# Cross attention's context keys and values: made per chunk in the cross stage, or for all chunks during the first chunks of attention and kept in memory

## The chip, the cores and the metric

One core of a Trainium2 chip. The metric is the device time of one execution in microseconds (us). Engines are named as in the profile: PE is TensorE's matrix multiplications and PEld its weight loads, DVE is VectorE, ACT ScalarE, POOL GpSimd, SP SyncE, which here issues most DMAs. Each engine runs its own instructions strictly in the order of its program and waits only on semaphores.

## What is computed

128 sequences of 64 tokens with 128 features (8192 tokens), all in f32, go through four residual steps. Cut to what matters:

```python
x = x + tanh(g_xattn[0]) * L0_xattn(layernorm(x), ctx)   # per token: 16 heads attend over each other
x = x + tanh(g_ffn[0])   * L0_ffn(layernorm(x))          # 2 of 8 experts, chosen by a sum of features
x = x + tanh(g_xattn[1]) * L1_xattn(layernorm(x), ctx)   # cross attention, 64 x 64 within a sequence
x = x + tanh(g_ffn[1])   * L1_ffn(layernorm(x))          # 2 shared units and 8 gated ones

# L1_xattn(vis, lang):
vis_key   = vis  @ W_vk.T + b_vk
lang_key  = lang @ W_lk.T + b_lk          # depends on the context alone
vis_value = vis  @ W_vv.T + b_vv
lang_value = lang @ W_lv.T + b_lv         # depends on the context alone
attn = softmax(vis_key @ lang_key.T * scale)
return attn @ lang_value + attn @ (attn.T @ vis_value)
```

The kernel computes the last line as attn @ (lang_value + attn.T @ vis_value).

## The kernel before

The tokens are cut into 16 chunks of 512 (`NC` = 16, `CH` = 512), four sequential 128-token tiles each. Four steps are staged over a common count of **half ticks** (`for half in range(2 * TICKS)`, with `tick = half // 2` and `later = half % 2`), and every engine runs its own copy of this loop. The order of the work on each engine is written out by these loops; engines meet only at semaphores, so a half tick is a place in the order and not a time.

- **Attention** (`a_part`, L95): chunk a takes half ticks 16(a+1) to 16(a+1)+15, and k is the place in it (0 to 15). The next chunk (p) and the one before (r) have places in the same sixteen. On PE (`attention`, `tail_uses` L119) k = 3 makes `ot` of chunk r (it waits for DVE's `head_scale`, L906, at k = 2) and the first half of keys and values of p, k = 5 makes `wo` of r (the output projection, L1341 and L1240) and the second half, k = 7 `xt0`, k = 10 `q`, k = 13 `rank`. DVE takes `wo` at k = 6 (`attended`, L913) to form the residual, and goes on with `norm_stats`; POOL needs these statistics at k = 8 (L562) before its products of the second half (L586).
- **Experts** of block b (four chunks): from half tick 108 (block 0) up to half tick 356, after a planned table (`PLACE`). Lines L1276 and L1290 on PE, L683 on ACT, L1014 on DVE. Their weights are loaded by SP.
- **Cross attention** of chunk c: from tick `C0[c]` = 136, 144, ..., 256, so 8 ticks for each chunk. PE's steps (`cross`, `C_FIRST` and `C_LATER`): `lk` (L1391, tick 0), `xt2` (tick 0, later half), `vk` (L1397, tick 1), `sc` (L1404, tick 1), `vv` (L1240, tick 2), `bdt`, `val` (L1415 and L1416 by turns, tick 4), `att` (L1422, tick 5), `xt3` (tick 7). ACT copies `lk` out of PSUM with its bias (L672). DVE adds the row bias to `val` (`biased`, L1019, into `u_sb`).
- **Units** of chunk c (the last step, 10 of them): from tick `C0[c]` + 8. PE L1244 to L1246 and L1326/L1328, ACT L705, DVE L1095 and L1110. DVE's `ut_lo` (L1188) comes ahead of unit 0.

The attention steps outside the experts and most cross steps share two PSUM banks, `M[0]` (MA) and `M[1]` (MC). `bank_uses` gives the cross steps these banks by turns, and each `fill` waits until the use before it in the same bank is drained. `ZB[0]` and `ZB[1]` are used for splitting the unit weights up to half tick 30 and then lie unused until the experts begin.

For cross attention SP loads chunk c of the context into `ctx2_t` (L515) two ticks ahead of `C0[c]`. The profile joins buffers whose names differ by numbers: `ctx_t` in its rows is also `ctx2_t`, `xn` also `xn2`.

## Time and profile before

| | us |
|---|---|
| runs (three) | 1303.09, 1305.31, 1306.69; median 1305.31 |
| the profiled execution's own time | 1305.32 |
| its span in the trace | 1303.6 |
| PE busy | 1113.0 (85%) |
| DVE busy | 1010.9 (78%) |
| ACT busy, POOL busy | 586.5 (45%), 637.0 (49%) |

Times in rows are counted from the span's start. A row of a timeline has: start us, us, engine, line, operation, out<-in, forms, count, and in brackets the idle time before it on its engine with what ended it. One f32 matrix multiplication is recorded as two. The rows of busy time by stretch give PE, PEld, DVE, ACT and POOL in this order, each with its instructions, then the clock. "PEclk" is the granted TensorE clock as a share of 2.4 GHz. For reading by time, four stretches: attention alone (to about 236 us), attention with experts (to about 630), experts with cross attention and units (to about 948), cross attention and units (to the end).

### The profile page before, as it was taken

The page shows a single profiled execution, that of the slowest core. Times are in us where ns is not written, and L with a number is a line of the kernel's source. Part 1 is how long each engine was busy: PE and PEld are TensorE (multiplying, and loading weights), DVE is VectorE, ACT ScalarE, POOL GpSimd, SP SyncE. Part 2 cuts the span into 40 slices and gives each one's busy share as a digit, 9 for nine tenths or more (in the row PEclk, how much of TensorE's full clock was granted, in tenths as well). Part 3 has the DMA queues.
Part 4 walks back from the last instruction along what each step waited for, and adds up shares of the span by engine and source line. Part 5 has one row for each costly group of instructions (what it writes and reads, how often), then busy time and mean ns, then how long its engine had stood idle before and what let it go on. Part 6 is the DMA issues. An engine that isn't in the chain of part 4 may idle for free.

```text
span 1303.6 us, 23736 instructions
## 1 busy us (share of the span) xinstructions
PE 1113.0 (85%) x7464; PEld 960.2 (74%) x7464; DVE 1010.9 (78%) x2393; ACT 586.5 (45%) x1506; POOL 637.0 (49%) x377
## 2 busy tenths in 40 slices
PE   5145544899969998799889999999999999999998
PEld 3133333789858988688788888889888888888887
DVE  2999999989999899898537444445688888888887
ACT  2212222465636555355454645454344444444443
POOL 4889997898788987899340110101011111111200
PEclk9999985799989999799899999999999999999999
DMA  6101112889748886589666255552000000000000
GB/s 226 49 25 41 40 41 73 264 269 284 224 151 263 278 253 208 187 240 294 189 198 206 78 176 160 174 162 79 22 25 25 25 25 25 26 25 25 26 9 17
DMA packets 125035, 166.41 MB, mean 128 GB/s; under 512 B 10032, under 2 KB 67568, under 8 KB 124912
## 3 DMA queue, kind: packets, MB, share of 16 engines
q1 hardware_dynamic: 119792, 152.31, 38.1%
q0 software_dynamic: 5120, 12.59, 2.9%
q8 instruction: 61, 1.00, 0.3%
q14 instruction: 62, 0.51, 0.1%
HBM read 137.60 MB, written 27.26 MB: 126 GB/s over the span
## 4 chain that ended last, share of the span: by engine, by line
PE 56%; DVE 25%; issue 8%; POOL 7%; ACT 2%; DMA 1%; SPq 0%; DVEq 0%; POOLq 0%; ACTq 0%
PE ZB L1276 8%; DVE q_sb L898 6%; PE YB L1290 6%; PE YD L1328 5%; DVE s L873 4%; PE ZD L1244 4%; PE ZD L1246 4%; PE ZD L1245 4%; POOL prod L586 3%; PE YB L1328 3%; PE ZB L1244 2%; DVE own_prod L862 2%; PE ZB L1246 2%; PE ZB L1245 2%; POOL xs L596 2%
## 5 line engine op out<-in xcount | busy, mean ns | idle before, releaser
L562 POOL TENSOR_TENSOR rstd<-ve,neghalf 128x4 f32<-128x4 f32 x64 | 65.6, 1025 | 516.6 <-DVE ve L827 515.2
L683 ACT ACTIVATE hid<-ZB,w2b 128x128 f32<-128x128 f32 x768 | 215.8, 378 | 159.0 <-PE YB L1290 78.5
L574 POOL TENSOR_TENSOR prod<-q_sb,kv_sb 128x2048 f32<-128x2048 f32 x48 | 216.3, 4507 | 51.9 <-DVE q_sb L898 31.6
L586 POOL TENSOR_TENSOR prod<-s,kv_sb 128x2048 f32<-128x2048 f32 x48 | 215.2, 4505 | 10.6 <-DVE q_sb L898 10.5
L1276 PE MATMUL ZB<-bt,w1b 128*128 128x128 f32 x1536 | 213.2, 284 | 4.9 <-ACT hid L683 4.7
L1276 PEld LDWEIGHTS ZB<-bt,w1b 128*128 128x128 f32 x1536 | 197.0, 200 | 8.5 <-issue 8.0
L1290 PE MATMUL YB<-w2b,hid 128*128 128x128 f32 x1024 | 141.4, 282 | 0.0
L1290 PEld LDWEIGHTS YB<-w2b,hid 128*128 128x128 f32 x1024 | 129.1, 194 | 14.2 <-ACT hid L683 8.0
L705 ACT ACTIVATE own_prod<-ZD 128x512 f32<-128x512 f32 x102 | 61.1, 599 | 154.6 <-PE ZD L1246 152.3
L1095 DVE TENSOR_TENSOR prod<-own_prod,ZD 128x512 f32<-128x512 f32 x102 | 69.5, 682 | 75.0 <-ACT own_prod L705 51.7
L1110 DVE SCALAR_TENSOR_TENSOR own_prod<-YD,gate,own_prod 128x128 f32<-128x128 f32 x320 | 89.7, 342 | 46.5 <-PE YD L1328 44.6
L873 DVE TENSOR_REDUCE s<-prod 128x256 f32<-128x2048 f32 x48 | 108.2, 2275 | 5.4 <-POOL prod L574 5.4
L898 DVE TENSOR_REDUCE q_sb<-prod 128x128 f32<-128x2048 f32 x48 | 109.1, 2273 | 1.4 <-POOL prod L586 1.0
L1244 PE MATMUL ZD<-ut_hi,w_hi 128*128 128x512 f32 x204 | 89.0, 436 | 0.0
L1328 PEld LDWEIGHTS YD<-w2u_sb,prod 128*128 128x128 f32 x640 | 79.8, 192 | 9.9 <-issue 4.7
L1328 PE MATMUL YD<-w2u_sb,prod 128*128 128x128 f32 x640 | 85.0, 276 | 2.4 <-DVE own_prod L1110 1.5
L1246 PE MATMUL ZD<-ut_lo,w_hi 128*128 128x512 f32 x204 | 80.5, 394 | 0.0
L1245 PE MATMUL ZD<-ut_hi,w_lo 128*128 128x512 f32 x204 | 80.4, 394 | 0.0
L596 POOL DMA_INDIRECT xs<-xrow,slots x64 | 63.3, 989 | 23.1 <-issue 17.7
L608 POOL DMA_INDIRECT x<-x2d,homes x64 | 61.8, 966 | 23.6 <-issue 23.3
L1290 PE MATMUL ZD<-w2b,hid 128*128 128x128 f32 x512 | 69.3, 279 | 0.0
L1290 PEld LDWEIGHTS ZD<-w2b,hid 128*128 128x128 f32 x512 | 62.6, 192 | 5.8 <-issue 3.0
(249 smaller groups left out, 2321.0 us busy)
## 6 DMA issues: line engine op xcount, KB each, us to landing
w2b<-in_w SPq DMA_DIRECT2D x96, 516.0 KB
w1b<-in_w SPq DMA_DIRECT2D x96, 512.0 KB
xb<-xs SPq DMA_DIRECT2D x96, 128.0 KB
ctx_t<-in_ctx SPq DMA_DIRECT2D x32, 256.0 KB
x2d<-x2s SPq DMA_DIRECT2D x48, 128.0 KB
x<-in_x SPq DMA_DIRECT2D x16, 256.0 KB
xs<-zrow SPq DMA_DIRECT2D x4, 1024.0 KB, 10.5
xrow<-in_x SPq DMA_DIRECT2D x16, 256.0 KB, 3.6
```

Of the source, the lines that this page charges most:

```text
L574: pool.tensor_tensor(out=prod[:, t % 2, :].rearrange("p (h e d) -> p h e d", h=HEADS, e=HEADS), in0=q.unsqueeze(2).broadcast_to([P, HEADS, ...
L586: pool.tensor_tensor(out=prod[:, (t + 1) % 2, :].rearrange("p (h d e) -> p h d e", h=HEADS, e=HEADS), in0=s0[:, t, :, :].unsqueeze(2).broa ...
L683: act.activation(hid[n % 2][:, j, k * RT:(k + 1) * RT], ZB[j // 2][:, at:at + RT], ACT.Relu, bias=w2b[t % 3][:, k, e, FJ * D + j:FJ * D + ...
L873: dve.tensor_reduce(out=s0[:, t, :, :].rearrange("p h e -> p (h e)"), in_=src.rearrange("p (g d) -> p g d", d=HD), axis=X, op=ALU.add).the ...
L898: dve.tensor_reduce(out=o_sb[a % 2][:, t, :], in_=src.rearrange("p (g e) -> p g e", e=HEADS), axis=X, op=ALU.add).then_inc(av_sum.sem, 1)
L1110: last = dve.scalar_tensor_tensor(out=xd[:, j, :], in0=b[:, j * P:(j + 1) * P], scalar=gate[:, j, u - SHARED:u - SHARED + 1], in1=xd[:, j, ...
L1244: pe.matmul(dst, l_hi, r_hi, start=True, stop=False)
L1245: pe.matmul(dst, l_lo, r_hi, start=False, stop=False)
L1246: return pe.matmul(dst, l_hi, r_lo, start=False, stop=True)
L1276: last = pe.matmul(ZB[j // 2][:, at:at + RT], w1b[t % 2][:, k, e, j * P:(j + 1) * P], bt[t % 2][:, k * RT:(k + 1) * RT], start=True, stop= ...
L1290: last = pe.matmul(b[:, k * D:(k + 1) * D], hid[n % 2][:, f, k * RT:(k + 1) * RT], w2b[t % 3][:, k, e, f * D:(f + 1) * D], start=False, st ...
L1328: last = pe.matmul(b[:, js], hu[(d * UNITS + u) % 3][:, js], w2u_sb[:, u, :], start=True, stop=True)
```

## The change

The two products that depend on the context alone, `lang_key` and `lang_value`, are taken out of the cross steps. A new step, `languages(c)`, makes both for chunk c at half tick 32 + 4c (`LANG`), that is at half ticks 32, 36, ..., 92, in the attention of chunks 1 to 4, at k = 0, 4, 8 and 12 of each. On PE it stands behind `attention(half)` of its half tick: one product for the keys into `ZB[0]`, then two bias rows and four products for the values into `ZB[1]`. ACT empties both one half tick later into `lk_t` and `vv_sb`, after the stores of the chunk before have landed. SP loads the context two half ticks ahead and stores both results into two DRAM tensors (`lk_d`, `lv_d`) two half ticks behind. In the cross stage SP then loads these two (256 KB each) in place of the context (256 KB); PE has no `lk` and no L1415 there; ACT has no `lk` copy; DVE adds the loaded values instead of the bias (`values`). As `lk` no longer takes a turn of the two banks, the turns of the steps behind it are swapped. The first expert products wait for the last `languages` (their banks are the same). The bias rows split in two parts reach 768 columns in place of 512.

```diff
--- before.py
+++ after.py
@@ -82,11 +82,14 @@
 XB = 4
 
 
+LANG = {32 + 4 * c: c for c in range(NC)}
+
+
 UNIT_IN = {1: 0, 2: 1, 4: 2, 5: 3, 7: 4, 8: 5, 10: 6, 11: 7, 13: 8, 14: 9}
 UNIT_OUT = {pos + 3: u for pos, u in UNIT_IN.items()}
 
 
-C_FIRST = {0: "lk", 1: "vk", 2: "vv", 4: "bdt"}
+C_FIRST = {1: "vk", 2: "vv", 4: "bdt"}
 C_LATER = {0: "xt2", 1: "sc", 4: "val", 5: "att", 7: "xt3"}
 
 
@@ -216,6 +219,7 @@
     x_v = x.rearrange("(c j p) d -> c p j d", j=TILES, p=P)
     out_v = out.rearrange("(c j p) d -> c p j d", j=TILES, p=P)
     xs = [nc.dram_tensor(f"xs{b}", (ROWS, 2 * D), F32, kind="Internal").ap() for b in range(len(BLOCKS))]
+    lk_d, lv_d = (nc.dram_tensor(n, (NC, P, CH), F32, kind="Internal").ap() for n in ("lk_d", "lv_d"))
     x2d = [nc.dram_tensor(f"x2d{b}", (NT[b] * RT, D), F32, kind="Internal").ap() for b in range(len(BLOCKS))]
 
     with ExitStack() as stack:
@@ -247,7 +251,7 @@
         upto, below = sb("upto", [1, E0, E0]), sb("below", [P, E0, E0])
         before = sb("before", [P, E1, E1])
         neghalf = sb("neghalf", [P, TILES])
-        ones_r, bias_hi, bias_lo = sb("ones_r", [1, P], F32R), sb("bias_hi", [1, BVV], F32R), sb("bias_lo", [1, BVV], F32R)
+        ones_r, bias_hi, bias_lo = sb("ones_r", [1, P], F32R), sb("bias_hi", [1, BG], F32R), sb("bias_lo", [1, BG], F32R)
         zrow = sb("zrow", [P, 2 * D])
 
 
@@ -293,7 +297,7 @@
         xn2 = sb("xn2", [P, TILES, D])
         xt2, ctx2_t, vk_t, lk_t = (sb(n, [P, CH]) for n in ("xt2", "ctx2_t", "vk_t", "lk_t"))
         vv_sb = sb("vv_sb", [P, TILES, D])
-        u_sb = vv_sb
+        u_sb, lv_sb = vv_sb, ctx2_t
         sc_sb = sb("sc_sb", [P, TILES, SEQ])
         mx1, sum1, rec1 = (sb(n, [P, TILES]) for n in ("mx1", "sum1", "rec1"))
         blockdiag, blockdiag_t = sb("blockdiag", [P, TILES, P]), sb("blockdiag_t", [P, TILES, P])
@@ -370,7 +374,8 @@
         st_x2 = [signal(f"st_x2_{i}", 16) for i in range(2)]
 
         ld_x2 = [signal(f"ld_x2_{j}", 16) for j in range(TILES)]
-        ld_cc = signal("ld_ctx_c", 16)
+        ld_cl, pe_lang, lang_s, st_lang = signal("ld_ctx_lang", 16), signal("pe_lang", 2), signal("lang_ready", 2), signal("st_lang", 32)
+        ld_lk, ld_lv = signal("ld_lk", 16), signal("ld_lv", 16)
         sub1, exp1, bd_s = signal("sub1"), signal("exp1"), signal("blockdiag_ready", 4)
 
         ut_hi_s = signal("ut_hi_ready")
@@ -507,12 +512,27 @@
                     store_x2(t)
                     if t + XB < NPAIRS and PBLOCK[t + XB] == PBLOCK[t]:
                         load_pair(t + XB)
+                if half + 2 in LANG:
+                    c = LANG[half + 2]
+                    if has(c - 1):
+                        sp.wait_ge(pe_lang.sem, pe_lang.at(c - 1))
+                    sp.dma_start(ctx2_t[:], ctx_in[:, c * CH:(c + 1) * CH]).then_inc(ld_cl.sem, 16)
+                if half - 2 in LANG:
+                    c = LANG[half - 2]
+                    sp.wait_ge(lang_s.sem, lang_s.at(c))
+                    sp.dma_start(lk_d[c], lk_t[:]).then_inc(st_lang.sem, 16)
+                    sp.dma_start(lv_d[c], vv_sb[:, :, :].rearrange("p j d -> p (j d)")).then_inc(st_lang.sem, 16)
                 if not later:
                     for c, k in c_parts(tick):
                         if k == -2:
                             if has(c - 1):
-                                filled(sp, "val", c - 1)
-                            sp.dma_start(ctx2_t[:], ctx_in[:, c * CH:(c + 1) * CH]).then_inc(ld_cc.sem, 16)
+                                filled(sp, "sc", c - 1)
+                            else:
+                                sp.wait_ge(st_lang.sem, st_lang.at(NC - 1))
+                            sp.dma_start(lk_t[:], lk_d[c]).then_inc(ld_lk.sem, 16)
+                            if has(c - 1):
+                                emptied(sp, "val", c - 1)
+                            sp.dma_start(lv_sb[:], lv_d[c]).then_inc(ld_lv.sem, 16)
                     for d in range(NC):
                         if tick == C0[d] + 17:
                             sp.wait_ge(xd_s.sem, xd_s.at(d))
@@ -647,7 +667,7 @@
                 act.wait_ge(s_pool, POOL_CONSTS)
                 act.activation(ones_r[:], ones[0:1, :], ACT.Copy)
                 act.wait_ge(s_rows, 16)
-                act.activation(bias_hi[:], brow[0:1, 0:BVV], ACT.Copy).then_inc(s_act0, 1)
+                act.activation(bias_hi[:], brow[0:1, 0:BG], ACT.Copy).then_inc(s_act0, 1)
 
             def normed(k, dst, src, c, js=range(TILES)):
                 act.wait_ge(ln_rstd[k].sem, ln_rstd[k].at(c))
@@ -737,6 +757,16 @@
                     plain(q_sb[p % 2][:, :, :].rearrange("p j d -> p (j d)"), "q", p)
                 if k == 11 and has(a):
                     exp_heads(a, 1)
+                if half - 1 in LANG:
+                    c = LANG[half - 1]
+                    if has(c - 1):
+                        act.wait_ge(st_lang.sem, st_lang.at(c - 1))
+                    else:
+                        act.wait_ge(raw_lo.sem, raw_lo.at(PIECES - 1))
+                    act.wait_ge(pe_lang.sem, pe_lang.at(c, 1))
+                    act.activation(lk_t[:], ZB[0][:], ACT.Identity, bias=bcol[:, CBLK:CBLK + 1]).then_inc(lang_s.sem, 1)
+                    act.wait_ge(pe_lang.sem, pe_lang.at(c))
+                    act.activation(vv_sb[:, :, :].rearrange("p j d -> p (j d)"), ZB[1][:], ACT.Copy).then_inc(lang_s.sem, 1)
                 made = place(half, 1)
                 if made is not None:
                     t, i = made
@@ -752,8 +782,6 @@
                             act.wait_ge(raw_lo.sem, raw_lo.at(i - 2))
                         act.activation(ZB[i % 2][:], hi.bitcast(F32), ACT.Copy).then_inc(raw_hi.sem, 1)
                     for c, kc in c_parts(tick):
-                        if kc == 0:
-                            with_bias(lk_t[:], "lk", c, CBLK)
                         if kc == 1:
                             with_bias(vk_t[:], "vk", c, CBVK)
                         if kc == 2:
@@ -807,7 +835,7 @@
                 dve.wait_ge(s_act0, 2)
                 step(dve.tensor_tensor(out=wg_parts[:, E1:2 * E1], in0=ws[:, WG:WSMALL], in1=wg_parts[:, 0:E1].bitcast(F32), op=ALU.subtract))
                 dve.wait_ge(s_act0, 3)
-                step(dve.tensor_tensor(out=bias_lo[:], in0=brow[0:1, 0:BVV], in1=bias_hi[:].bitcast(F32), op=ALU.subtract))
+                step(dve.tensor_tensor(out=bias_lo[:], in0=brow[0:1, 0:BG], in1=bias_hi[:].bitcast(F32), op=ALU.subtract))
                 dve.wait_ge(s_dve0, DVE_CONSTS)
                 dve.wait_ge(s_rows, 16)
 
@@ -1018,6 +1046,11 @@
                 b = filled(dve, *use)
                 dve.tensor_tensor(out=dst[:], in0=tiles(b), in1=brow[:, row:row + D].unsqueeze(1).broadcast_to([P, TILES, D]),
                                   op=ALU.add).then_inc(free_of(*use), 1)
+
+            def values(c):
+                b = filled(dve, "val", c)
+                dve.wait_ge(ld_lv.sem, ld_lv.at(c))
+                dve.tensor_tensor(out=u_sb[:], in0=tiles(b), in1=tiles(lv_sb), op=ALU.add).then_inc(free_of("val", c), 1)
 
             def score_max(c):
                 b = filled(dve, "sc", c)
@@ -1207,7 +1240,7 @@
                         if kc == 2:
                             score_parts(c)
                         if kc == 4:
-                            biased(BLV, u_sb, "val", c)
+                            values(c)
                         if kc == 5:
                             residual3(c)
                     for d, kd in d_parts(tick):
@@ -1270,6 +1303,8 @@
                 pe.wait_ge(ld_w1[t % 2].sem, ld_w1[t % 2].at(t // 2))
                 if n > 0:
                     pe.wait_ge(relu_s.sem, relu_s.at(n - 1, SUB * (js[-1] + 1)))
+                else:
+                    pe.wait_ge(lang_s.sem, lang_s.at(NC - 1))
                 for j in js:
                     for k in range(SUB):
                         at = (j % 2) * SUB * RT + k * RT
@@ -1375,6 +1410,17 @@
                     if name == "totals":
                         pe.matmul(b[:, 0:E0], ones[:], run_end[:], start=True, stop=True).then_inc(full(name, c), 1)
 
+            def languages(c):
+
+                if has(c - 1):
+                    pe.wait_ge(lang_s.sem, lang_s.at(c - 1))
+                else:
+                    pe.wait_ge(raw_lo.sem, raw_lo.at(PIECES - 1))
+                pe.wait_ge(ld_cl.sem, ld_cl.at(c))
+                pe.matmul(ZB[0][:], ws[:, WLK:WLK + P], ctx2_t[:], start=True, stop=True).then_inc(pe_lang.sem, 1)
+                bias_rows_of(ZB[1][:, :], BLV, D, TILES)
+                by_token(ZB[1], ctx2_t, WLV, D, start=False).then_inc(pe_lang.sem, 1)
+
             def cross(name, c):
                 b = fill(name, c)
                 done = full(name, c)
@@ -1386,9 +1432,6 @@
                         pe.matmul(b[:, cols], ut_hi[c % 2][:, js], wg_parts[:], start=True, stop=False)
                         last = pe.matmul(b[:, cols], ut_lo[c % 2][:, js], wg_high[:], start=False, stop=True)
                     last.then_inc(done, 1)
-                if name == "lk":
-                    pe.wait_ge(ld_cc.sem, ld_cc.at(c))
-                    pe.matmul(b[:], ws[:, WLK:WLK + P], ctx2_t[:], start=True, stop=True).then_inc(done, 1)
                 if name == "xt2":
                     pe.wait_ge(ln_done[2].sem, ln_done[2].at(c))
                     transposes(b, xn2).then_inc(done, 1)
@@ -1397,7 +1440,7 @@
                     pe.matmul(b[:], ws[:, WVK:WVK + P], xt2[:], start=True, stop=True).then_inc(done, 1)
                 if name == "sc":
                     emptied(pe, "vk", c)
-                    emptied(pe, "lk", c)
+                    pe.wait_ge(ld_lk.sem, ld_lk.at(c))
                     for j in range(TILES):
                         for h in range(2):
                             ts = slice(j * P + h * SEQ, j * P + (h + 1) * SEQ)
@@ -1412,8 +1455,7 @@
                     emptied(pe, "vv", c)
                     for j in range(TILES):
                         js = slice(j * P, (j + 1) * P)
-                        pe.matmul(b[:, js], ctx2_t[:, js], ws[:, WLV:WLV + D], start=True, stop=False)
-                        last = pe.matmul(b[:, js], blockdiag[:, j, :], vv_sb[:, j, :], start=False, stop=True)
+                        last = pe.matmul(b[:, js], blockdiag[:, j, :], vv_sb[:, j, :], start=True, stop=True)
                     last.then_inc(done, 1)
                 if name == "att":
                     emptied(pe, "bdt", c)
@@ -1439,6 +1481,8 @@
                 for t in sorted_next(half):
                     sorted_t(t)
                 attention(half)
+                if half in LANG:
+                    languages(LANG[half])
                 stages = C_LATER if later else C_FIRST
                 for c, kc in c_parts(tick):
                     if kc in stages:
```

## Rows read from the trace of the kernel before

**Rows 1.** The page: PE's busy tenths and its granted clock in 40 equal slices

```profile
PE   5145544899969998799889999999999999999998
...
PEclk9999985799989999799899999999999999999999
```

**Rows 2.** Busy us by stretch: window, length, engines in order, clock, DMA share, GB/s

```profile
56.00:196.00 140.00, 66.06 (x200) 45.85 (x200) 134.95 (x211) 28.39 (x60) 128.79 (x53) 0.96 0.11 34
...
686.00:940.00 254.00, 248.48 (x1841) 221.75 (x1840) 130.64 (x402) 125.85 (x335) 25.26 (x32) 1.00 0.45 135
960.00:1283.00 323.00, 314.78 (x2122) 272.79 (x2121) 262.70 (x860) 151.60 (x265) 54.20 (x70) 1.00 0.08 23
```

**Rows 3.** The same view: PE's busiest part of three attention chunks

```profile
63.00:79.00 16.00, 14.59 (x40) 9.51 (x40) 15.38 (x29) 6.07 (x14) 13.63 (x7) 1.00 0.17 50
...
168.00:184.00 16.00, 13.18 (x40) 8.49 (x40) 15.38 (x29) 5.29 (x12) 14.16 (x11) 0.99 0.21 67
208.00:224.00 16.00, 14.51 (x40) 9.51 (x40) 15.35 (x30) 5.05 (x11) 14.15 (x11) 0.50 0.31 99
```

**Rows 4.** Timeline of all engines, attention chunk 1, k = 2 to 6

```profile
63.40 1.09 PE L1235 MATMUL MA<-ident,q_sb 128*128 128x128 f32 x4 [20.55 <-DVE q_sb L906]
...
67.56 0.79 PE L1341 MATMUL MA<-bias_hi,ones_r 1*128 1x512 f32 x1
...
68.71 2.08 PE L1240 MATMUL MA<-ws,ot 128*128 128x128 f32 x8
...
70.72 0.79 PE L1341 MATMUL MC<-bias_hi,ones_r 1*128 1x512 f32 x1
...
70.90 0.75 DVE L913 SCALAR_TENSOR_TENSOR xrow<-MA,tg,xrow 128x512 f32<-128x512 f32 x1 [0.34 <-PE MA L1240]
```

**Rows 5.** DVE's L913 from 60 to 230: idle in total, times

```profile
  PE MA L1240: 1.7, 5
```

**Rows 6.** PE's timeline at full clock: one projection of attention chunk 15

```profile
645.64 0.49 PE L1341 MATMUL MA<-bias_hi,ones_r 1*128 1x512 f32 x1
...
647.29 1.06 PE L1290 MATMUL ZD<-w2b,hid 128*128 128x128 f32 x8
```

**Rows 7.** PE's timeline at the beginning of cross chunk 0

```profile
629.95 2.08 PE L1391 MATMUL MA<-ctx_t,ws 128*128 128x512 f32 x2 [5.78 <-DVE spick L950]
631.81 1.91 PE L1276 MATMUL ZB<-bt,w1b 128*128 128x128 f32 x8
633.52 1.01 PE L1235 MATMUL MC<-ident,xn 128*128 128x128 f32 x4
```

**Rows 8.** ACT's timeline there

```profile
625.15 1.65 ACT L655 ACTIVATE xn<-x,nmr,rstd 128x128 f32<-128x128 f32 x4 [1.76 <-POOL nmr L564]
```

**Rows 9.** What PE waited for from 690 to 922, the largest: total, times, longest

```profile
PE ZB L1276 <- ACT hid L683: 1.6, 3, 0.7
```

**Rows 10.** PE's timeline in one steady period of the last stretch

```profile
1227.31 0.38 PE L1415 MATMUL MC<-ws,ctx_t 128*128 128x128 f32 x2
...
1229.10 1.06 PE L1328 MATMUL YB<-w2u_sb,prod 128*128 128x128 f32 x8
...
1231.39 1.05 PE L1422 MATMUL MA<-vv_sb,blockdiag_t 128*128 128x128 f32 x8
```

**Rows 11.** PE's timeline at that period's end

```profile
1239.58 1.02 PE L1391 MATMUL MA<-ctx_t,ws 128*128 128x512 f32 x2
1240.44 1.05 PE L1328 MATMUL YB<-w2u_sb,prod 128*128 128x128 f32 x8
1242.05 0.63 PE L1235 MATMUL MC<-ident,xn 128*128 128x128 f32 x4 [0.56 <-DVE ut_lo L1188]
```

**Rows 12.** DVE in that period: timeline

```profile
1230.38 0.68 DVE L1019 TENSOR_TENSOR vv_sb<-MC,brow 128x512 f32<-128x512 f32 x1
```

**Rows 13.** ACT in that period: timeline

```profile
1240.27 1.64 ACT L655 ACTIVATE xn<-x,nmr,rstd 128x128 f32<-128x128 f32 x4
```

**Rows 14.** Busy us in that period up to the end of DVE L1188

```profile
1220.30:1242.20 21.90, 21.34 (x141) 18.73 (x141) 21.23 (x73) 8.81 (x19) 2.45 (x4) 1.00 0.05 13
```

## The prediction

> **What bounds the kernel now.** I read the page's slices first, then busy time by stretch, then the timeline at the places that the change touches. PE is about half busy in the first fifth of the span and nearly full behind it [rows 1]. The change takes work out of the full part and puts it into the half-empty part, and that looks like a plain gain. Three stretches say more.
>
> In attention alone, DVE is busy 134.95 of 140 us and PE only 66.06 [rows 2]: DVE sets the pace (34.8 us for a chunk), POOL is next, and PE waits for DVE. But PE is not free of the path at every point. In each attention chunk PE gets DVE's last result at 63.40, works from there without a pause through `ot`, the first keys and values and `wo` to 70.72, and DVE, which has done its own steps in between, waits 0.34 us for `wo` [rows 4]. It does so in all five chunks seen from 60 to 230, 1.7 us in total [rows 5]. So this one stretch of 7.3 us on PE has no slack at all.
>
> From 686 to 940 PE is busy 248.48 of 254 us and DVE 130.64 [rows 2]; the largest thing that PE waited for there comes to 1.6 us in all [rows 9]. PE is the bound.
>
> From 960 on PE is busy 314.78 of 323 us, yet DVE has 262.70 [rows 2]. In a steady period (32.3 us a chunk) DVE is busy 21.23 of 21.90 us in one piece from unit 2 to its `ut_lo` [rows 14], and at the end of that piece PE waits 0.56 us [rows 11]. Both engines are on a loop there: the DVE piece, then a piece of PE work that holds neither `lk` nor L1415.
>
> **The level of the clock.** The granted clock prints 1.00 for 63 to 79 us and 0.50 for 208 to 224, but PE and PEld have the same busy time for the same 40 instructions in both (14.59 and 9.51 against 14.51 and 9.51) [rows 3]. So PE runs at 1.2 GHz in both; the column is not to be trusted ahead of its first change. The group of two bias rows and four projections takes 3.16 us there (67.56 to 70.72) [rows 4] and 1.65 us at the full 2.4 GHz (645.64 to 647.29) [rows 6].
>
> **What the change adds: `languages`.** One call is a keys product and such a group for the values. The keys product took 1.86 us at the low level (629.95 to 631.81) [rows 7] and 0.86 at the full one (1239.58 to 1240.44) [rows 11]. So one call costs 1.86 + 3.16 = 5.02 us of PE at 1.2 GHz, 0.86 + 1.65 = 2.51 at 2.4.
>
> Four calls fall into each of the attention chunks 1 to 4. The one at k = 4 stands, in PE's program, behind `ot` and the first keys and values (k = 3) and ahead of `wo` (k = 5): right inside the stretch without slack. DVE's wait at L913 grows from 0.34 us by the whole call. Behind that waiting instruction stand all of DVE's statistics and the rest of the chunk's reductions, and POOL's second half waits for these statistics; neither has other work to do. Cost: 4 x 5.02 = 20.1 us. Its bounds are nothing (the clock has risen, below) and 20.1; I take 20.1: in the fourth chunk the same 40 instructions took 13.18 us, so a part ran at the full level, but in the first and the fifth all of it ran low [rows 3] (the two between are like the first).
>
> The calls at k = 0, 8 and 12 I cost at nothing. At k = 0 PE otherwise waits for `head_scale` (20.55 us in the first of these chunks [rows 4]); at k = 12 it would wait for DVE's expert choice. At k = 8 the call delays `q`, used only sixteen half ticks on, and ACT, which empties `ZB` at k = 9 before it normalizes for DVE's k = 12; by the sum that leaves about 1 to 2 us of slack. PE's load in a chunk becomes 16.4 (66.06 x 34.8 / 140) plus 20.1, that is 36.5 us of a chunk of now 39.8: it fits. If that cover is gone, each of the twelve costs up to 5.02.
>
> Also at nothing: 16 context loads moved forward and 32 stores, with the DMA share at 0.11 in that stretch [rows 2]. SP waits for ACT's copy before the stores, and queued behind are the loads of `ctx_t`, `x0` and `xrow`, all needed many half ticks on. ACT (28.39 of 140 us [rows 2]) waits for the stores of the call before, issued three half ticks earlier. The loads of `lk` and values in the cross stage are 256 KB more a chunk, issued at least two ticks ahead on SP, past the expert weights, at DMA shares of 0.45 and 0.08 [rows 2]; if late, `sc` on PE would wait. The larger bias rows cost only start-up time on one partition. DVE's addition of loaded values in place of a bias keeps its size of 0.68 us [rows 12]; bounds -0.1 and +0.1 us a chunk, nothing taken.
>
> **What it removes.** On PE per chunk: `lk` 0.86 us [rows 11] and four L1415; eight products of L1415 and L1416 by turns take 1.79 us (1227.31 to 1229.10), so half of that, 0.90 [rows 10]. Together 1.76 us. What of it comes back:
> - Chunk 0. `lk` waits 5.78 us for a bank, then takes 1.86, and an expert step behind it 1.71, before `xt2` at 633.52 [rows 7]. What `xt2` reads was ready at 625.15 + 1.65 = 626.80 [rows 8]. Without `lk` the expert step goes ahead of the wait and `xt2` inherits it (same bank, by the turns): up to 3.57 us. But PE ran at the low level there, and will for some time after any such wait; at full clock the two are 0.86 and some 0.9. Between 1.8 and 3.6 I take 2.5. With 0.9 for L1415: 3.4.
> - Chunks 1 to 4, PE-bound: 4 x 1.76 = 7.0.
> - Chunk 5, half within either regime: 0.9 of its 1.76.
> - Chunks 6 to 15. The 0.90 saved in `val` brings PE earlier to `att` (1231.39 [rows 10]), but `att` needs DVE's addition, which ends at 1230.38 + 0.68 = 1231.06 [rows 12] in the piece that DVE works through without a pause. With some 0.09 us from release to start, `att` moves by 0.24 at most, and all behind it by as much. The 0.86 of `lk` falls into a wait: `xt2` starts at 1242.05 [rows 11] since ACT's normalization ends at 1240.27 + 1.64 = 1241.91 [rows 13]; PE will wait 1.4 us there instead of 0.56. So 10 x 0.24 = 2.4. Bounds: 0 and the full 17.6.
>
> Sum of the gains: 3.4 + 7.0 + 0.9 + 2.4 = 13.7 us, bounds 9 and 30.
>
> **The forecast.** The profiled execution took 1305.32 us, the median of the three runs is 1305.31, so the sum holds for both: 1305.3 + 20.1 - 13.7 = 1311.7, about 1312.
>
> **Rivals.**
> 1. *The clock rises because of the added work.* PE would be busy over 90% in the attention of chunks 1 to 4 instead of 47%, and once, in the fourth of those stretches, its work did go over to the full level on the way [rows 3]. From 63.40 to `wo`'s end PE would then need some 0.5 + 1.65 + 2.51 + 1.65 = 6.3 us against 7.3 now: no cost, and the 0.34 us waits go too. 1305.3 - 13.7 - 1.4 = 1290. Against it: before each such stretch PE still waits for DVE, and after waits of that kind it is low. If half of the four calls are paid: 1305.3 + 10 - 13.7 = 1302.
> 2. *PE alone is the bound to the end,* as 97% busy suggests: then chunks 6 to 15 give 17.6 in place of 2.4 and chunk 5 its full 1.76. 1311.7 - 16.1 = 1296. Against it: DVE's unbroken piece [rows 14].
> 3. *The cover at k = 0, 8 and 12 is thinner than I count* (ACT waits for stores or for PE, DVE's expert choice or `rank` comes late): from about 2 us of further delay in each chunk it decides. At 2 us a chunk 1320, at most 60 us more.
>
> The Trainium skill, "TensorE: Matmul & The Clock Gate", Part 1 on the clock gate, says that the low clock is the default state and that activity releases it. By that rule rival 1 would hold and the time be 1290. The trace agrees that waits precede the low level, but not that a busy PE suffices: 14.59 busy us of 16 stayed low [rows 3].
>
> **How the numbers follow.** Chances: forecast 0.45; half of the calls paid 0.17; rival 1 in full 0.10; rival 2 0.13; rival 3 0.15. The range takes in rival 2 and the low end of rival 3 and leaves out rival 1 in full and the far end of rival 3: 1294 to 1320. A change under 0.3% (3.9 us) can't be told from none. Slower by more: rival 3 and most of the forecast, 0.50; within: the half-paid case and the forecast's lower edge, 0.21; faster: rivals 1 and 2 and a rest, 0.29.
>
> **What would show it.** In the changed kernel's profile: DVE's L913 waiting about 5.3 us for PE in four attention chunks and 0.34 in the fifth; attention chunks of 39.8 us instead of 34.8 from 56 to 216; the keys product at k = 4 at about 0.9 us a record and not 0.6; PE from 686 to 940 shortened by some 7 us; periods of 32.1 us instead of 32.3 at the end, with PE waiting 1.4 us ahead of `xt2`. Wrong would be the prediction if L913 does not wait, if the last periods shrink by more than 1 us, or if DVE waits elsewhere in attention.

## The result: where the time went

| | kernel before | changed kernel |
|---|---|---|
| median, us | 1306.56 (20 runs, 1303.09 to 1309.27) | 1311.14 (20 runs, 1305.53 to 1316.95) |
| ratio to before | | 1.0037, 95% interval 1.0023 to 1.0051 |
| the profiled execution, its span | 1305.32, 1303.6 | 1312.46, 1310.2 |
| PE, DVE busy | 1113.0, 1010.9 | 1139.4, 1010.3 |

The changed kernel is 0.37% slower; 1312 was predicted. Its runs spread over 11.4 us, those of the kernel before over 6.2.

The page's slices of the changed kernel [rows 1 of before] show PE filled up in the second to sixth slice, where the calls stand:

```profile
PE   5378774699987999699889899999999999999998
...
PEclk9986775799987999889899999999999999999999
```

Busy time by stretch (window, length, PE, PEld, DVE, ACT, POOL, clock, DMA share, GB/s) [rows 2]:

```profile
56.00:196.00 140.00, 105.37 (x372) 66.59 (x372) 124.88 (x197) 44.97 (x88) 121.20 (x52) 0.73 0.37 119
686.00:940.00 254.00, 246.58 (x1811) 221.43 (x1811) 124.05 (x381) 126.63 (x339) 28.36 (x36) 0.98 0.47 143
960.00:1283.00 323.00, 302.61 (x2030) 260.11 (x2029) 263.77 (x864) 145.86 (x256) 54.64 (x71) 1.00 0.11 31
```

In attention PE is busy 105 us instead of 66, and DVE, which sets the pace there, only 124.88 instead of 134.95: ten microseconds in which it waits. In the last stretch PE has 12.2 us less to do, and DVE is as busy as before.

What DVE waited for from 60 to 230, its attended rows (L941, L913 before) [rows 5]:

```profile
DVE xrow L941 <- PE MA L1273: 7.7, 4, 2.7
DVE xrow L941 <- issue: 5.2, 1, 5.2
```

Before, this was 1.7 us in five waits. The timeline of PE in attention chunk 2 of the changed kernel shows the longest, and DVE's line behind it (start, us, what, and the idle time before it):

```profile
101.02 1.09 PE L1268 MATMUL MA<-ident,q_sb 128*128 128x128 f32 x4 [4.00 <-DVE q_sb L934]
...
103.19 2.08 PE L1273 MATMUL MC<-ws,ctx_t 128*128 128x256 f32 x4
105.06 1.91 PE L1420 MATMUL ZB<-ctx_t,ws 128*128 128x512 f32 x2
106.90 0.79 PE L1376 MATMUL ZB<-bias_hi,ones_r 1*128 1x512 f32 x1
107.50 0.62 PE L1376 MATMUL ZB<-bias_lo,ones_r 1*128 1x512 f32 x1
108.05 2.08 PE L1273 MATMUL ZB<-ws,ctx_t 128*128 128x128 f32 x8
110.05 0.79 PE L1376 MATMUL MA<-bias_hi,ones_r 1*128 1x512 f32 x1
```

```profile
113.39 0.75 DVE L941 SCALAR_TENSOR_TENSOR xrow<-MA,tg,xrow 128x512 f32<-128x512 f32 x1 [5.21 <-issue]
```

The call takes 105.06 to 110.05, 4.99 us at 1.2 GHz, and DVE's wait is 5.21: the mechanism and the price of the prediction. (The profile names no releaser for this one wait, "issue"; L941 starts 0.11 us behind the end of `wo`'s last product, 111.20 + 2.08, as it does in the chunks where PE is named.) But in chunk 1 the level changed in the middle of the call:

```profile
67.90 1.91 PE L1420 MATMUL ZB<-ctx_t,ws 128*128 128x512 f32 x2
69.74 0.79 PE L1376 MATMUL ZB<-bias_hi,ones_r 1*128 1x512 f32 x1
70.33 0.45 PE L1376 MATMUL ZB<-bias_lo,ones_r 1*128 1x512 f32 x1
70.71 1.16 PE L1273 MATMUL ZB<-ws,ctx_t 128*128 128x128 f32 x8
...
72.46 1.16 PE L1273 MATMUL MA<-ws,ot 128*128 128x128 f32 x8
```

The same four products (eight records, x8) last 1.16 us and not 2.08, and `wo` behind them too; the call costs 3.90 us and `wo` gives back 1.5. DVE waits 2.70.

The distance of the two traces (start of the same instruction in the changed kernel less that in the one before, so read off both timelines), at PE's `ot` in attention and at `vk` in the cross stage, in us. `ot` is numbered by the sixteen half ticks in which it stands (k = 3); `ot` 1 stands ahead of every call at k = 4, and at `ot` 5 attention alone ends. Each row is one profiled execution, and those of one kernel differ by several microseconds (e3's was the fastest of its six, 4.5 us below their median). Up to `vk` 5 the changed kernel, e4 and e7 run the same instructions:

```
                    ot 1   ot 2   ot 5   ot 9  ot 13  ot 15 | vk 0   vk 2   vk 5   vk 6   vk 15
changed kernel       0.5    2.8   10.1   11.0   13.9   13.8 | 11.3   13.1    7.8    6.9    6.7
e4_late_double      -0.9    0.8    8.0    8.0    9.4    8.0 |  7.5   10.0    4.7    3.8    3.8
e7_dve_twice         0.7    5.5   12.7   12.8   14.2   12.8 | 10.3   11.0    5.8    4.9   10.1
e3_cross_alone      -1.3   -1.3   -1.3   -1.2   -1.0   -2.4 | -4.9   -5.5  -10.8  -11.7  -11.9
e6_without_k4        0.5    0.6    0.7    0.8    0.8    0.8 |  0.9    3.7   -1.6   -2.5   -2.6
e2_calls_only       -0.9    3.9   11.0   11.3   13.8   13.8 | 13.8   15.5   15.4   15.4   15.6
e8_two_sets          0.5    3.1    4.4    4.5    4.5    4.5 |  3.3    3.7   -1.5   -2.4   -2.6
e9_free_places      -1.0   -1.0   -0.1   -0.3    0.6    0.6 | -0.1    0.4   -4.7   -5.6   -5.9
e10_filler           0.6    1.6    3.1    3.4    3.4    2.0 |  1.2    1.6   -3.5   -4.4   -4.7
e11_before_filler    0.1    0.1    0.2    0.1    1.4    0.0 |  1.4    1.4    1.4    1.4    1.5
e12_free_filler      0.0   -1.1   -0.5   -0.4   -0.5   -1.9 | -2.2   -2.7   -7.9   -8.8   -8.9
```

For the changed kernel: +10.1 in attention alone (0.5 of it already there at `ot` 1), +3.8 while the experts run beside it, -2.5 at cross chunk 0, -4.4 from there to chunk 6, and then almost nothing for ten chunks. The rows of e4 and e7 say how far one execution can be trusted: the same code gave 8.0 and 12.7 at `ot` 5, 0.0 and +0.1 from there to `ot` 15, and -0.4 and -2.5 at cross chunk 0.

### The profile page after: what moved, and what is told of

Its sections match the earlier page's. It is cut to its first block, busy times and chain, and to the rows that moved or that the text cites. A ratio compares the mean times of both kernels' runs of the same rounds, so it can differ in the third digit from the quotient of the medians.

```text
span 1310.2 us, 23912 instructions
## 1 busy us (share of the span) xinstructions
PE 1139.4 (87%) x7496; PEld 969.0 (74%) x7496; DVE 1010.3 (77%) x2393; ACT 595.4 (45%) x1522; POOL 637.1 (49%) x377
## 4 chain that ended last, share of the span: by engine, by line
PE 56%; DVE 31%; issue 7%; POOL 3%; ACT 2%; DMA 1%; SPq 0%; DVEq 0%; another core or an unknown queue 0%; POOLq 0%; ACTq 0%
PE ZB L1311 9%; PE YB L1325 6%; DVE q_sb L926 6%; DVE s L901 5%; PE YD L1363 4%; PE ZD L1277 3%; PE ZD L1279 3%; PE ZD L1278 3%; PE YB L1363 2%; PE MC L1273 2%; PE ZD L1325 2%; DVE own_prod L890 2%; DVE own_prod L882 2%; PE MA L1273 2%; PE ZB L1277 2%
## 5 line engine op out<-in xcount | busy, mean ns | idle before, releaser
L1311 PE MATMUL ZB<-bt,w1b 128*128 128x128 f32 x1536 | 214.7, 286 | 10.1 <-ACT hid L703 7.9
L1325 PE MATMUL YB<-w2b,hid 128*128 128x128 f32 x1024 | 144.1, 285 | 0.0
L1143 DVE SCALAR_TENSOR_TENSOR own_prod<-YD,gate,own_prod 128x128 f32<-128x128 f32 x320 | 89.9, 345 | 46.1 <-PE YD L1363 45.3
L725 ACT ACTIVATE own_prod<-ZB 128x512 f32<-128x512 f32 x58 | 34.7, 598 | 71.9 <-PE ZB L1279 71.6
```

The source lines that it names most:

```text
L725: act.activation(su[:, u % 2, :], unit_pair[PAIR[d, u][0]][0][:], ACT.Silu).then_inc(silu_s.sem, 1)
L1311: last = pe.matmul(ZB[j // 2][:, at:at + RT], w1b[t % 2][:, k, e, j * P:(j + 1) * P], bt[t % 2][:, k * RT:(k + 1) * RT], start=True, stop= ...
L1325: last = pe.matmul(b[:, k * D:(k + 1) * D], hid[n % 2][:, f, k * RT:(k + 1) * RT], w2b[t % 3][:, k, e, f * D:(f + 1) * D], start=False, st ...
```

## The experiments

Theory A: the four calls at k = 4 sit on the path to DVE, and the level of PE's clock there sizes them; the other twelve are free; in the cross stage PE's saving counts until DVE's loop takes over. Theory B: what is paid in attention comes from the sheer number of calls, loads and stores. All ratios are to runs of the kernel before on the same chip.

### The four calls one half tick later

```diff
-LANG = {32 + 4 * c: c for c in range(NC)}
+LANG = {32 + 4 * c + (c % 4 == 1): c for c in range(NC)}
```

> The changed kernel with one edit: the call of languages at k = 4 of each of the four attention chunks stands one half tick later, that is behind wo in PE's order instead of ahead of it; all the work is the same. Theory A (the cost lies in this one place: the call delays wo, and DVE waits for it, 12.5 us in total at L941 instead of 1.4): these waits go back to about 0.35 us each and the kernel gains about 11 us on the changed one, some 1300 us. Theory B (the cost is in the calls' work as such, through ACT, SP, the DMAs or the PSUM banks, wherever it stands): no gain, about 1311 us.

Measured: 1310.04 us, 1.0017 (1.0002 to 1.0033). A miss by 10 us: the time is the one that Theory B gives, but not by its cause. The wait that I wanted gone is gone, and others stand in its place. DVE's waits from 60 to 230:

```profile
DVE YD L952 <- ACT xrow L675: 7.8, 3, 4.6
DVE oh_all L950 <- ACT xrow L675: 3.3, 1, 3.3
DVE xrow L941 <- PE MA L1273: 2.2, 5, 0.8
```

and PE's in the same stretch:

```profile
PE ZB L1420 <- DMA ctx_t<-in_ctx: 16.6, 8, 3.1
```

The next call is now three half ticks behind. There is one context buffer, so its load can't start before this call ends, and PE stands before a load (16.6 us in eight waits, against 5.0 in four in the changed kernel): at k = 8 of all four chunks, 9.8 us together, ahead of `q` and the rest, and four times at k = 12 or 0, while ACT, in its order behind the copies of `ZB`, normalizes late for DVE. Moving a step changed its distance to its neighbour as much as its distance to the path.

### Calls without their use, and their use without the calls

```diff
# e2: cross steps as before the change; calls, loads and stores kept (one line of the edit;
# the cross stage's own `lk`, its values, loads and bias are put back in the same way)
-C_FIRST = {1: "vk", 2: "vv", 4: "bdt"}
+C_FIRST = {0: "lk", 1: "vk", 2: "vv", 4: "bdt"}
# e3: no calls (of its two loads in the cross stage the first; the second likewise)
-LANG = {32 + 4 * c: c for c in range(NC)}
+LANG = {}
-                            sp.dma_start(lk_t[:], lk_d[c]).then_inc(ld_lk.sem, 16)
+                            sp.dma_start(lk_t[:], ctx_in[:, c * CH:(c + 1) * CH]).then_inc(ld_lk.sem, 16)
```

> The kernel before with the first half of the change alone: the sixteen calls with their loads, copies and stores are made, but cross attention doesn't use them and makes its keys and values itself as before (the stored ones are never read). Theory A: before plus the 11 us of waits at L941 plus up to 3 us that attention with experts lost as well, 1317 to 1321 us. Rival (the calls cost little and it is the cross stage that fails to gain): 1307 to 1311 us.

> The other half alone: cross attention as changed, but nothing is made in attention; the two loads of a chunk read the context instead of the made keys and values (so the output is another). By my prediction's own sum it gains 13.7 us: 1293 us. By the trace of the changed kernel, in which the distance to the kernel before shrinks only by 7 us behind attention, 1299 us, and 1296 if the longer low-clock spells there came from the calls. By the rival that PE is the bound to the end it would be 1277 us.

Measured: e2 1319.16 us, 1.0078 (1.0053 to 1.0102); e3 1297.83 us, 0.9924 (0.9910 to 0.9938). e2 came out as expected (1317 to 1321), e3 between the three figures that I had put down. The kernel before had a median of 1307.02 beside them, so the calls cost 12.1 us and their use gives 9.2; the changed kernel's +4.6 lies near their sum, 2.9. Of the 28 us that PE is spared (16 x 1.76), nine arrive. e3's distances show where: -4.9 at `vk` 0 (-1.3 of it was there at `ot` 1, ahead of anything that the edit is about, and -2.5 came at cross chunk 0 itself), -6.7 from there to chunk 6, -0.2 in the last nine periods together.

### The four calls at k = 4 alone, and the twelve others alone

```diff
# e5 (both: chunks that no call serves load the context in place of keys and values)
+LANG = {h: c for c, h in enumerate([36, 52, 68, 84])}
# e6
+LANG = {h: c for c, h in enumerate([h for h in range(32, 96, 4) if h % 16 != 4])}
```

> The cross stage as changed with the calls at k = 4 alone: four calls of the sixteen, at half ticks 36, 52, 68 and 84; for the other twelve chunks cross attention reads the context itself (another output). To be read against the cross stage without any call (0.9924 of the kernel before, 1297 us) and the changed kernel (1.0037). Theory A (the calls at k = 4 carry the cost): 5.0 us of wait each at the low clock, since with so few calls PE stays low: 4 x 4.9 = +20 us on 1297, that is 1313 to 1319 us, more than the changed kernel with all sixteen. Theory B (the whole load of calls carries it): a quarter of 13 us, about 1300.

> The complement: the twelve calls at k = 0, 8 and 12, none at k = 4 (the last four chunks read the context). As I costed them in the prediction, these calls are free: 1297 us, L941 waiting 0.35 us. Theory C, which the kernel with the call behind wo suggests (the calls of the middle of the chunk hold up q on PE and with it the softmax on ACT and the products on POOL; in the changed kernel the stall at k = 4 covers for it): 3 to 11 us more, 1300 to 1308 us, with POOL waiting for ACT's L719 and DVE for ACT's L675.

Measured: four calls 1309.38 us, 1.0021 (1.0004 to 1.0038); twelve calls 1300.04 us, 0.9956 (0.9942 to 0.9969). DVE's waits from 60 to 230, first with the four alone:

```profile
DVE xrow L942 <- PE MA L1274: 12.1, 5, 5.2
```

and with the twelve:

```profile
DVE xrow L942 <- PE MA L1274: 1.7, 5, 0.4
DVE q_sb L927 <- POOL prod L607: 0.8, 4, 0.2
```

A quarter of the calls makes all of the wait, and three quarters leave the kernel before's 1.7 us untouched; `ot` of chunks 2 to 5 stands 0.6 to 0.7 us late, of which 0.5 was there at `ot` 1. Theory B falls. Each taken from the kernel before beside it (+2.8 and -6.5) and set against e3's -9.2, the four cost 12.0 us and the twelve 2.7, little of it in these attention chunks.

e5's own figure was a miss, 1309.38 against 1313 to 1319. I had reasoned that with so few calls PE stays at the low level and all four are paid in full. PE idled 20.55 us ahead of `ot` in chunk 1 and 9.06 to 9.07 ahead of the next three, and yet DVE's waits were 2.02, 2.51, 5.20 and 2.00: the level rose within the call in three of four. So a long idle time ahead of `ot` doesn't keep the call at the low level; `ot` itself ran low in all four (1.09 us).

The size differs from run to run of the same code. In attention the changed kernel and the next two experiments (whose edits lie far behind it) run the same instructions, and their waits in chunks 1 to 4, by DVE's timeline, were 2.70, 5.21, 2.02, 2.59; then 2.07, 2.54, 5.20, 2.02; then 5.20, 2.52, 5.20, 2.01. Attention alone cost 10.1, 8.0 and 12.7 us, or from `ot` 1 on 9.6, 8.9 and 12.0. A call paid in full appears as 5.2, one in which the level rises as 2.0 to 2.7. That is where the changed kernel's wider spread can come from.

### What bounds the last ten chunks

```diff
# e4: val of chunks 6 to 15 (shown) and the output of unit 8 (the same edit) each made twice
-                    for j in range(TILES):
+                    for j in range(2 * TILES if c >= 6 else TILES):
+                        j %= TILES
# e7: DVE's addition made twice
             def values(c):
                 b = filled(dve, "val", c)
                 dve.wait_ge(ld_lv.sem, ld_lv.at(c))
+                if c >= 6:
+                    dve.tensor_tensor(out=xn2[:], in0=tiles(b), in1=tiles(lv_sb), op=ALU.add)
```

> The changed kernel with PE work put back in the last stretch alone: for chunks 6 to 15 the four products of val and the four of the output of unit 8 (which stands where lk stood) are made twice, some 1.7 us of PE in each of ten periods, 17 us in all, with no other engine's work changed. Theory A (a loop through DVE sets the period): under 2 us more than the changed kernel, since the doubled products fall into PE's waits. Rival (PE is the bound there): 17 us more, about 1328 us.

> The changed kernel with DVE's addition at val (L1053, 0.69 us) made twice in chunks 6 to 15, nothing else. Theory A (the steady period of the last stretch is a loop that runs through an unbroken piece of DVE work): every period grows by what DVE takes for it, 0.6 us, together 6 us: 1317 us. Rival (PE sets the period, or both have slack): no change, 1311 us. The doubled PE work of three times that size (17 us) cost less than 1 us at the same place.

Measured: e4 1310.33 us, 1.0028 (1.0014 to 1.0042), no more than the changed kernel's 1311.14 although PE was busy 316.85 us there from 960 to 1283 (the changed kernel: 302.61). e7 1317.64 us, 1.0085 (1.0068 to 1.0102), 6.5 us more than the changed kernel for ten additions of 0.68. In this stretch 14 us more of PE cost nothing and 6.8 of DVE are paid almost in full: rival 2 is refuted, and it is explained why PE's saving yields so little there.

### Other places for the calls

With two sets of buffers (context, keys, values) a call no longer waits for the stores and the load of the one before, so calls may stand two half ticks apart. e8 and e9 differ in the places alone:

```diff
# e8
+LANG = {h: c for c, h in enumerate([32, 34, 43, 44, 46, 48, 59, 60, 62, 64, 75, 76, 78, 91, 92, 94])}
# e9
+LANG = {h: c for c, h in enumerate([32, 34, 40, 44, 48, 56, 60, 64, 72, 76, 80, 88, 92, 96, 98, 104])}
# both
+        lang_c = [ctx2_t, xt2]
+        lang_k = [lk_t, vk_t]
+        lang_v = [vv_sb, xn2]
# (and the loads, copies, stores and semaphores by turns of two)
```

> All sixteen calls, at places where PE has nothing urgent: half ticks 32 and 34, then k = 11, 12 and 14 of the attention chunks 1 to 4 and k = 0 of two of them, with two sets of buffers (context, keys, values) in place of one, so that a load need not wait for the call before. If the cost lies only in the places (theories A and C together), attention costs 0 to 4 us and the kernel comes to 1297 to 1302 us, below the kernel before. If sixteen calls cost in any place, about 1308 to 1311 us.

> All sixteen calls, nothing left out, as in the changed kernel; but the context loads alternate between two sets of buffers, and the calls stand at halves 32, 34, 40, 44, 48, 56, 60, 64, 72, 76, 80, 88, 92, 96, 98, 104, that is at places behind which no output of the attention follows at once, spread over five chunks. If what a call costs is only where it stands (Theory A), the attention's chunks keep their times to within 2 us as with the twelve calls alone (1300.04), the waits of the attended rows stay at 0.35 us each, and the cross attention gives its 7 back: 1298 to 1301 us. Rival: calls cost wherever sixteen of them stand, by making the output projection of the next half late: waits of 1 to 5 us in at least two chunks and 1303 to 1307 us.

Measured: e8 1306.46 us, 1.0008 (0.9988 to 1.0028), a miss by 4.5 us. e9 1301.24 us, 0.9959 (0.9944 to 0.9975). In e8 a call at k = 14 and one at k = 0 stand shortly before `ot`; in two chunks PE came late to it and DVE waited 0.82 us where the level rose right behind `ot` and 4.79 where it stayed low. Its DVE waits:

```profile
DVE xrow L949 <- PE MA L1281: 6.3, 4, 4.8
```

In e9 the same row is

```profile
DVE xrow L949 <- PE MA L1281: 2.5, 5, 1.1
```

and attention alone costs nothing (-0.1). It has all sixteen calls, twelve of them in the old half ticks and four in 34, 96, 98 and 104 in place of 36, 52, 68 and 84, and is 0.4% below the kernel before, where the changed one was 0.4% above it. "Outside the stretch" was not enough for e8: PE's whole work up to `ot` has to fit too. Against the changed kernel e9 changes two things, the places and the second set of buffers, and no run has its places with one set; that the four places carry most of the cost rests on e5 and e6.

### The level of the clock ahead of the call

```diff
                 attention(half)
                 if half in LANG:
                     languages(LANG[half])
+                if half - 2 in LANG and half % 16 == 2:
+                    pe.wait_ge(lang_s.sem, lang_s.at(LANG[half - 2]))
+                    for _ in range(2):
+                        pe.matmul(ZB[0][:], ws[:, 0:P], ws[:, 0:CH], start=True, stop=True)
```

> The changed kernel, nothing left out, with two more products of 128 by 512 (about 0.4 to 0.9 us of TensorE) into a PSUM buffer that nobody reads, in half k = 2 of each of the four chunks, ahead of the attention's output projection. It is more work on TensorE. If the clock level at which the call at k = 4 runs decides the size of the wait (Theory A), and filling TensorE's idle time ahead of it raises the level, the waits of the attended rows shrink from 12.5 us in total to about 8 (2 each), and the time from 1311 to about 1307 us. If the clock isn't reached by so small a filling, or doesn't decide, there is no gain: 1311 to 1314 us and waits of 12 to 16 us in total.

Measured: 1301.04 us, 0.9962 (0.9947 to 0.9978). Eight products that nobody reads, two a chunk, bring the changed kernel from 4.6 us above the kernel before to 5.0 below it. They are larger than I had put down: 3.51 to 3.78 us a pair, not 0.4 to 0.9. PE's timeline in chunk 2, to be held against the one from 101.02 on above:

```profile
96.39 3.58 PE L1489 MATMUL ZB<-ws 128*128 128x512 f32 x4 [0.69 <-ACT vv_sb L769]
99.80 0.60 PE L1268 MATMUL MA<-ident,q_sb 128*128 128x128 f32 x4
...
100.99 1.13 PE L1273 MATMUL MC<-ws,ctx_t 128*128 128x256 f32 x4
101.96 1.02 PE L1420 MATMUL ZB<-ctx_t,ws 128*128 128x512 f32 x2
...
103.57 1.16 PE L1273 MATMUL ZB<-ws,ctx_t 128*128 128x128 f32 x8
```

```profile
106.78 0.74 DVE L941 SCALAR_TENSOR_TENSOR xrow<-MA,tg,xrow 128x512 f32<-128x512 f32 x1
```

The products fill all but 0.69 of the 4 us that PE idled before `ot`, everything from `ot` on runs at 2.4 GHz, and the chain from `ot` to DVE's L941 takes 6.98 us with the call in it, against 12.37 in the changed kernel and 7.51 before without one. DVE does not wait at all. Chunk 4 was like chunk 2. In chunk 3 `ot` still ran low (1.09 us) and the level rose within the keys product; in chunk 1, where PE idled 1.48 us between the products and `ot`, `ot` ran at the full level (0.63), the keys product of the call low (1.92) and the rest full again. DVE waited 2.30 and 1.29 us there. Attention alone cost 3.1 us instead of 10.1. I had expected a gain of 4 us and measured 10.

Is that the filling's own doing, or the calls'? The same products in the kernel before, and in e9:

```diff
# e11, the kernel before
+                if half in (34, 50, 66, 82):
+                    pe.wait_ge(raw_lo.sem, raw_lo.at(PIECES - 1))
+                    for _ in range(2):
+                        pe.matmul(ZB[0][:], ws[:, 0:P], ws[:, 0:CH], start=True, stop=True)
# e12, e9 with the same lines, waiting for lang_s
```

> The kernel before, nothing left out, with the two unread products of the previous kernel in the same four halves (k = 2 of chunks 1 to 4) and no calls. In the kernel before DVE waits only 0.34 us for the attended rows in each chunk, so if the filling helped only by shortening the wait that the call at k = 4 makes (Theory A), the kernel before gains nothing from it: 1304 to 1308 us, within 0.2% of 1306. If the filling helps by itself, because a higher clock makes the whole attention faster, the kernel before gains as the changed kernel did: 1295 to 1300 us, and then the 10 us belong to the filling and not to the calls.

> The sixteen calls at the free places with two buffer sets (1301.24 us), nothing left out, with the same filling in halves 34, 50, 66 and 82. There the waits of the attended rows are already 2.5 us in all. By Theory A no gain is left for the filling in attention's first chunks: 1300 to 1303 us. If the filling also keeps later chunks out of low clock, or helps by itself, 1290 to 1298 us; if PE's added work makes the rows late, 1304 to 1308.

Measured: e11 1306.92 us, 1.0008 (1.0000 to 1.0017): no gain, as expected. e12 1297.00 us, 0.9930 (0.9916 to 0.9944), 4.2 us below e9 and the lowest median of all kernels here, in part of which work was left out. For e12 I had expected 1300 to 1303 by Theory A; it fell into the range of "keeps later chunks out of low clock, or helps by itself". But e11 is a weaker control than I meant. Without a call before them the products ran early and PE idled again (5.46 to 7.22 us), and `ot` stayed at the low level in all four chunks:

```profile
89.10 3.76 PE L1445 MATMUL ZB<-ws 128*128 128x512 f32 x4
98.31 1.08 PE L1235 MATMUL MA<-ident,q_sb 128*128 128x128 f32 x4 [5.46 <-DVE q_sb L906]
```

It shows that the products gain nothing by being there, not what a high level would do without calls. That is bounded by other rows: before, DVE waits 0.34 us a chunk in that place [rows 5], and e12, at the full level there but for a part of `ot`, is 1.1 us ahead of the kernel before by `ot` 2 and 0.5 by `ot` 5. One or two microseconds, then, of the nine or ten. Of e12's lead on e9 only 0.4 us is there at `ot` 5; 1.7 arise from `ot` 5 to `vk` 0, where the two kernels have the same instructions at other times, and 1.0 in the first cross period, where the granted clock was 0.93 in e12 and 0.91 in e9; no run says why.

## Why the prediction was right, point by point

The sum came within a microsecond, but not because its terms did.

- **A call at k = 4 lands in DVE's wait: right.** e5 against e6 shows it, and 4.99 us for a call at 1.2 GHz (5.02 predicted) with a wait of 5.21 (5.36).
- **20.1 us for four: mis-sized; 10.1 measured** (8.0 and 12.7 in the two other kernels with this code, 12.0 by e5's and e3's medians). I had priced all four at the low level, because waits precede the stretch. The row that should have made me choose a middle was there: the fourth stretch before, 13.18 against 14.59 us [rows 3], had the level rise on its way (behind `wo`), and the call lengthens PE's work, so more of it comes behind such a rise. The case "half of the calls paid" (0.17) was this term's right value. The Trainium skill, "TensorE: Matmul & The Clock Gate", Part 1, says that activity releases the low clock. The traces agree only in part: filled up to `ot`, the stretch ran at the full level throughout in e10's chunks 2 and 4, but in its chunk 3, filled the same way, it began low; and after 4.00 us of idling it stayed low in the changed kernel's chunk 2 from 101.02 us on, with PE busy all 12.00 us from 103 to 115 and a granted clock of 0.50, while in chunks 3 and 4 the level rose within the call after the same 4.00.
- **Twelve calls at nothing: right** in attention (e6: 0.2 us from `ot` 1 to `ot` 5), and 2.7 us in all by the medians of e6 and e3.
- **Attention beside the experts at nothing: +3.8 in the changed kernel's profiled execution, but 0.0 and +0.1 in e4 and e7**, which run the same instructions there (`ot` 5 to `ot` 15). So the 3.8 isn't shown to be a cost of the change. The same stretch up to `vk` 0, and so with chunk 0's gain in it, gave +1.2 in the changed kernel, e3 -3.7, e4 -0.4, e6 +0.2, e7 -2.4, e8 -1.0, e9 0.0, e10 -1.9, e12 -1.7, and without that gain e2 +2.8 and e11, in which nothing of the change was made, +1.2. So a few microseconds come and go there from one execution to the next. Spells of low clock shift in the same places, but no run separates cause and effect.
- **Chunk 0's wait for a bank: 2.5 predicted, 2.5 measured** (the distance falls from 13.8 to 11.3 there), and the exact agreement is luck. From `ot` 15 to `vk` 0 e7 and e3 gave 2.5 too, but e4, with the changed kernel's code, 0.4, e1 1.8, and e5, e6, e8, e9, e10 and e12 between -0.1 and 1.2; e11, without the change, lost 1.4 there.
- **From `vk` 0 to `vk` 6: 8.8 predicted** (0.9 of chunk 0's `val`, 7.0, 0.9), **4.4 measured.** The periods behind `vk` 2, 3 and 4 gave 1.70, 1.78 and 1.76: PE-bound, as priced, to a few hundredths, and the next 0.91, as guessed. But the first two gave nothing and lost 0.3 and 1.5. In the second (`vk` 1 to 2) PE waited for ACT and came back at the low level:

```profile
736.07 2.05 PE L1311 MATMUL ZB<-bt,w1b 128*128 128x128 f32 x8 [2.38 <-ACT hid L703]
```

(the four products, x8, take 1.06 otherwise). In other runs this level goes with the sign. The second period took 45.3 us before; in kernels with the same work in the cross stage it came in two lengths, 46.7 to 46.8 us at a granted clock of 0.96 (changed kernel, e1, e4 to e8) and 44.4 us at 1.00 (e3, e9, e10, e12). Window, length and busy times, first of the changed kernel, then of e3:

```profile
695.50:742.30 46.80, 42.92 (x299) 38.20 (x298) 29.07 (x90) 21.83 (x53) 6.31 (x8) 0.96 0.54 167
679.30:723.70 44.40, 41.30 (x299) 36.57 (x298) 29.07 (x90) 21.72 (x53) 6.31 (x8) 1.00 0.59 179
```

At the full level the period gave 0.9 and not 1.76, with a wait of 1.6 us for ACT's `hid` in it. The first period goes with the clock in the same way: 46.6 us at 1.00 (e8), 47.0 at 0.96 (e7), 48.0 at 0.93 (changed kernel), 49.1 at 0.91 (e9), and 47.7 at 0.96 before. What brings these low spells about no run isolates.
- **Chunks 6 to 15: 2.4 predicted, 0.2 measured** over nine periods. The regime was right (e4, e7), the detail wrong. I let PE keep `val`'s 0.90 us up to `att` and gave `att` 0.24 of it. But right behind `val` stands a unit's output product, and it reads what DVE's L1095 has just made. In the kernel before:

```profile
1228.16 0.68 DVE L1095 TENSOR_TENSOR prod<-own_prod,ZD 128x512 f32<-128x512 f32 x1
```

which ends at 1228.84; the product came at 1229.10 [rows 10]. So it could come at most 0.26 us earlier, of the 0.90 saved ahead of it. In the changed kernel:

```profile
1234.06 1.05 PE L1458 MATMUL MA<-vv_sb,blockdiag 128*128 128x128 f32 x8
1235.72 1.13 PE L1363 MATMUL YB<-w2u_sb,prod 128*128 128x128 f32 x8 [0.61 <-DVE prod L1128]
...
1238.09 1.05 PE L1464 MATMUL MC<-vv_sb,blockdiag_t 128*128 128x128 f32 x8
...
1248.74 0.63 PE L1268 MATMUL MC<-ident,xn 128*128 128x128 f32 x4 [1.06 <-ACT xn L675]
```

From `val` to `att` it is 4.03 us now and was 4.08: a gain of 0.05, where the periods shrank by 0.03 (all nine) to 0.06 (without the first). The wait before `xt2` grew from 0.56 to 1.06 and not to 1.4 as the saving of `lk` would have it, so part of that went to another wait.

So the calls cost half of the term and the cross stage gave half of its own: +20.1 - 13.7 = +6.4 against +10.1 + 3.8 - 2.5 - 4.4 - 0.2 = +6.8 for the two profiled executions (+7.1 by their own times). By the medians it is 4.6. The two errors, each of them several microseconds, cancelled; that the total came out is luck, and says little about its terms.

Of what the prediction named as signs: L941 waiting 5.3 us in four chunks came once in four; the fifth waited 0.34; the periods did not reach 32.1; 686 to 940 was shorter by 5.2 us from `vk` 2 to `vk` 5, of 7 expected over it all.

## What to carry to other kernels

Idle time of an engine says how much work fits, not where: work that is moved into it must end before the next instruction that another engine is waiting for, and its neighbours' buffers must be free by then. Price a step by the place, by what stands right ahead of and behind it in program order, and ask of each microsecond saved whose result the very next instruction reads; with a second set of buffers and four of the sixteen calls in other half ticks, +0.4% became -0.4%. And where PE idles ahead of a short stretch on the path, count that stretch at both levels of the clock, since the call in it cost 2.0 to 5.2 us of waiting from one execution to the next. And before a term is booked as measured, look at a second execution of the same code: here three of them differed by up to 4.7 us in attention and by 2 us at one cross chunk.

## What the runs showed of the hardware

Eight more f32 products of 128 by 512 (two a chunk, 3.5 to 3.8 us), placed right ahead of a stretch on the path (without a gap in three chunks, with one of 1.48 us in the other), brought `ot` and what follows to 2.4 GHz in two of four chunks and part of it in the others, and the changed kernel's median from 1311.14 to 1301.04 us: added work on the engine that was late made it less late. The same products followed by 5.46 to 7.22 us of idling left `ot` at the low level. The granted clock's column prints 1.00 for 63 to 79 us in the changed kernel:

```profile
63.00:79.00 16.00, 15.13 (x57) 9.12 (x57) 13.02 (x29) 6.78 (x14) 11.28 (x7) 1.00 0.25 83
```

In that window the four products (x8) of L1273 took 1.16 us at 70.71 and the keys product before them 1.91, which is 1.02 at 2.4 GHz: ahead of its first change the column can't be used, and the durations of one repeated form tell the level instead.
